# Every other partition for each of a pair's two primitives, and feed-forward biases loaded in attention

## The reference, cut to what matters

```python
def _compose_weight(logits, A, B):
    vals, idx = jax.lax.top_k(logits, 32)
    w = jax.nn.softmax(vals / 1.0)
    return jnp.einsum('k,kir,kro->io', w, A[idx], B[idx])   # A: (64, d_in, 64), B: (64, 64, d_out)

W1 = _compose_weight(fc1_logits, fc1_A, fc1_B)              # (256, 1024)
W2 = _compose_weight(fc2_logits, fc2_A, fc2_B)              # (1024, 256)
h = gelu(x @ W1)
return h @ W2
```

## Time and profile before

| | us |
|---|---|
| median of 3 runs (lowest, highest) | 1976.05 (1974.21, 1977.6) |
| the profiled execution | 1973.82 |
| its span, first to last instruction | 1972.0 |
| PE busy in the span | 1919.5 (97%) |
| DVE, ACT, POOL busy | 1345.8, 981.2, 1068.6 |
| mean granted TensorE clock | 0.988 of 2.4 GHz |

### The profile page before, as it was taken

How to read it: one execution, slowest core, us unless ns; L and a number is a source line. 1 busy time by engine, 2 the same in 40 slices (tenths; PEclk the granted TensorE clock), 3 DMA queues, 4 the chain that set the end, 5 groups by cost and what they waited for, 6 DMA issues and landing times.

```text
span 1972.0 us, 47533 instructions
## 1 busy us (share of the span) xinstructions
PE 1919.5 (97%) x19756; PEld 1579.7 (80%) x19756; DVE 1345.8 (68%) x3293; ACT 981.2 (50%) x1803; POOL 1068.6 (54%) x973
## 2 busy tenths in 40 slices
PE   8998999999999999999999879999999999999998
PEld 2335888888888888888888679999999999999997
DVE  3555566676667666776677655869686868777776
ACT  4444666776767666766676543222323222322231
POOL 1453998899889998899889201222212121312221
PEclk9997999999999999999999989999999999999999
DMA  7344200022000300021102864101010101010100
GB/s 274 123 162 164 107 34 34 34 76 76 34 34 3 117 34 34 34 76 55 34 15 69 221 160 109 44 23 43 33 35 31 44 22 44 22 44 22 44 11 22
DMA packets 26247, 128.04 MB, mean 65 GB/s; under 512 B 4592, under 2 KB 5168, under 8 KB 19888
## 3 DMA queue, kind: packets, MB, share of 16 engines
q1 hardware_dynamic: 19952, 86.53, 13.7%
q0 software_dynamic: 2304, 25.17, 3.8%
q10 hardware_dynamic: 3776, 13.30, 1.7%
HBM read 93.53 MB, written 31.46 MB: 63 GB/s over the span
## 4 chain that ended last, share of the span: by engine, by line
PE 81%; POOL 3%; DMA 2%; issue 2%; DVE 1%; ACT 1%; SPq 1%; POOLq 0%; ACTq 0%; DVEq 0%
PE bankC L32 12%; PE bankC L34 12%; PE bankC L33 12%; PE ring L32 6%; PE ring L34 6%; PE ring L33 6%; PE big L877 4%; PE big L32 3%; PE big L34 3%; PE big L33 3%; PE ring L808 3%; PE big L788 3%; PE big L884 3%; PE ring L852 2%; PE ring L830 2%
## 5 line engine op out<-in xcount | busy, mean ns | idle before, releaser
L32 PE MATMUL bankC<-down_hi,act_hi 128*128 128x256 f32 x1024 | 292.1, 285 | 0.0
L34 PE MATMUL bankC<-down_hi,act_lo 128*128 128x256 f32 x1024 | 289.5, 283 | 0.0
L33 PE MATMUL bankC<-down_lo,act_hi 128*128 128x256 f32 x1024 | 288.8, 282 | 0.0
L1490 DVE TENSOR_TENSOR act_lo<-gel,act_hi 128x512 fp32r<-128x512 f32 x256 | 210.6, 823 | 8.8
L1452 POOL TENSOR_TENSOR rstdC<-var_epsC,minus_halfC 128x4 f32<-128x4 f32 x48 | 53.9, 1122 | 281.5 <-DVE var_epsC L1515 281.5
L32 PE MATMUL bankC<-aT_hi,up_hi 128*128 128x512 f32 x512 | 204.1, 399 | 0.0
L34 PE MATMUL bankC<-aT_hi,up_lo 128*128 128x512 f32 x512 | 201.7, 394 | 0.0
L1446 POOL TENSOR_TENSOR hC<-hC,vecC 128x1024 f32<-128x1024 f32 x16 | 39.5, 2470 | 298.0 <-PE turn L1363 298.0
L33 PE MATMUL bankC<-aT_lo,up_hi 128*128 128x512 f32 x512 | 200.7, 392 | 0.0
L33 PEld LDWEIGHTS bankC<-down_lo,act_hi 128*128 128x128 f32 x1024 | 195.5, 191 | 1.4
L32 PEld LDWEIGHTS bankC<-down_hi,act_hi 128*128 128x128 f32 x1024 | 194.8, 190 | 1.4
(11 more groups left out here) (192 smaller groups left out, 5398.6 us busy)
## 6 DMA issues: line engine op xcount, KB each, us to landing
w_first<-w_split POOLq DMA_DIRECT2D x8, 1536.0 KB, 7.1
w_second<-w_split POOLq DMA_DIRECT2D x8, 1536.0 KB, 8.7
raw_late<-in_AB SPq DMA_DIRECT2D x30, 320.0 KB, 5.1
xs<-in_x_conv SPq DMA_DIRECT2D x16, 513.0 KB, 7.5
u<-hA SPq DMA_DIRECT2D x8, 1024.0 KB, 4.6
u_next<-u SPq DMA_DIRECT2D x8, 1024.0 KB, 6.0
hC<-u SPq DMA_DIRECT2D x16, 512.0 KB, 3.9
xC<-in_x SPq DMA_DIRECT2D x16, 512.0 KB, 4.8
```

Source lines behind the costliest of these rows:

```text
L32: e.matmul(out, wh, xh, start=start, stop=False)
L33: e.matmul(out, wh, xl, start=False, stop=False)
L34: return e.matmul(out, wl, xh, start=False, stop=stop)
L1490: e.tensor_tensor(a_lo[:, fb, :], g, a_hi[:, fb, :].bitcast(F32), ALU.subtract).then_inc(s_act_lo, 1)
```

## The change

Three things change.

1. Of a pair's two primitives one fills the even partitions and the other the odd ones (`to[half::2, :]`). `w_col` must follow: `vector_rest` makes a column of ones on even and one on odd partitions (`parity`) by a sum over the identity matrix, for which it waits, and forms `w_col` with six instructions in place of four. The constant `ROW` moves up by one, since one more instruction counts the semaphore up.
2. `b1s` and `vecC` get memory of their own, and their two DMAs move from ACT's list at n = 12 to SP's list, ahead of the loads of pair 0 in `prefetch`. The wait for all of attention moves to just before `first.scalar`.
3. `first.scalar(0)` and `first.vector(0)` move from n = 14 to n = 16.

```diff
--- before.py
+++ after.py
@@ -325,7 +325,8 @@
             rank.vector(e)
             for n in range(STEPS + LAG):
                 if n == LAG:
-                    rank.vector_rest(e)
+                    w.wait_ge(d_eye, 16)
+                    rank.vector_rest(e, identity)
                 if 0 <= n - LAG < STEPS:
                     keep_rows(n - LAG)
                 q, half = half_at(n)
@@ -363,6 +364,7 @@
         self.chosen, self.ones, self.euler = sb("chosen", [N, 2]), sb("onesN", [N, P]), sb("euler", [N, 2])
         self.weight, self.place = sb("weight", [N, 2, P]), sb("place", [N, 2, K])
         self.inv_sum, self.total, self.w_row = sb("inv_sum", [P, 2]), sb("total", [P, 2]), sb("w_row", [P, 2, K])
+        self.parity = sb("parity", [P, 2])
         sem = lambda n: ctx.enter_context(nc.semaphore("rank_" + n))
         self.d_in, self.s_ones, self.s_v, self.s_exp, self.s_mm = (sem(n) for n in ("in", "ones", "v", "exp", "mm"))
 
@@ -382,10 +384,10 @@
         e.wait_ge(self.s_v, self.LESS_TOP)
         e.tensor_tensor(self.expo[:, :], self.euler[:, :], self.expo[:, :], ALU.pow).then_inc(self.s_exp, 1)
 
-    LESS_TOP, PLACES, ROW = 9, 14, 15
+    LESS_TOP, PLACES, ROW = 9, 14, 16
 
     def vector(self, e):
-        v, K, R = self.s_v, self.K, P // 2
+        v, K = self.s_v, self.K
         e.wait_ge(self.d_in, 4 * 16)
         for f in range(2):
             e.tensor_scalar(self.more[:, f, :], self.row[:, f, :], self.col[:, f:f + 1], None, ALU.is_gt).then_inc(v, 1)
@@ -410,22 +412,28 @@
             e.tensor_scalar(self.place[:, f, :], self.index[:, 1:1 + K], self.rank[:, f:f + 1], None,
                             ALU.is_equal).then_inc(v, 1)
 
-    def vector_rest(self, e):
-        v, K, R = self.s_v, self.K, P // 2
+    def vector_rest(self, e, identity):
+
+        v, K = self.s_v, self.K
+        e.tensor_reduce(self.parity[:, :], identity[:, :].rearrange("p (a two) -> p two a", two=2), X, ALU.add).then_inc(v, 1)
         e.wait_ge(self.s_mm, 1)
         e.tensor_copy(self.w_row[:, :, :].rearrange("p a b -> p (a b)"), self.rows_ps[:, 0:2 * K]).then_inc(v, 1)
         e.tensor_copy(self.picks[:, :], self.picks_ps[0:1, 0:2 * K]).then_inc(v, 1)
-        e.wait_ge(v, 15)
+        e.wait_ge(v, 16)
         e.tensor_reduce(self.total[:, :], self.w_row[:, :, :], X, ALU.add).then_inc(v, 1)
-        e.wait_ge(v, 17)
+        e.wait_ge(v, 18)
         e.reciprocal(self.inv_sum[:, :], self.total[:, :]).then_inc(v, 1)
-        e.wait_ge(v, 18)
+        e.wait_ge(v, 19)
+        at = lambda f, half: self.w_row[:, f, :].rearrange("p (a two) -> p a two", two=2)[:, :, half]
         for f in range(2):
-            for half in range(2):
-                rows = slice(R * half, R * half + R)
-                e.tensor_scalar(self.w_col[rows, f, :],
-                                self.w_row[rows, f, :].rearrange("p (a two) -> p a two", two=2)[:, :, half],
-                                self.inv_sum[rows, f:f + 1], None, ALU.mult).then_inc(v, 1)
+            e.tensor_scalar(self.w_col[:, f, :], at(f, 1), self.parity[:, 1:2], None, ALU.mult).then_inc(v, 1)
+        for f in range(2):
+            e.wait_ge(v, 21 + f)
+            e.scalar_tensor_tensor(self.w_col[:, f, :], at(f, 0), self.parity[:, 0:1], self.w_col[:, f, :], ALU.mult,
+                                   ALU.add).then_inc(v, 1)
+        for f in range(2):
+            e.wait_ge(v, 23 + f)
+            e.tensor_scalar(self.w_col[:, f, :], self.w_col[:, f, :], self.inv_sum[:, f:f + 1], None, ALU.mult).then_inc(v, 1)
 
     def tensor(self, e):
         K = self.K
@@ -1169,7 +1177,7 @@
 
 
 def ffn_phase(nc, x, u_in, out, w1, b1, w2, rows2, comp, identity, w_col, picks, place, sems, before, early,
-              d_early, d_u4, x1_at, y_at):
+              d_early, d_consts, d_u4, x1_at, y_at):
     B, T, H = x.shape
     F = w1.shape[1] // (H // P)
     CB, FB = H // P, F // P
@@ -1188,13 +1196,12 @@
 
         up = [split("up0", [P, CB, F]), split("up1", [P, CB, F])]
         down = [split("down0", [P, FB, H]), split("down1", [P, FB, H])]
-        b1s = sb("b1s", [P, FB + 2 * CB])
-        vec = sb("vecC", [P, 5 * H])
+        b1s, vec = place["b1s"], place["vecC"]
         minus_half = sb("minus_halfC", [P, TILES])
         x_both, h_both = place["xC"], place["hC"]
         gel = sb("gel", [P, GEL, TOK])
         hs = [h_both[:, s, :, :] for s in range(LANES)]
-        d_consts, d_w, d_h = sem("d_consts"), [sem(f"d_w{n}") for n in range(2)], [sem(f"d_h{s}") for s in range(LANES)]
+        d_w, d_h = [sem(f"d_w{n}") for n in range(2)], [sem(f"d_h{s}") for s in range(LANES)]
         rows = lambda a: a.rearrange("p t c -> p (t c)")
         h_rows = u_in.rearrange("b p (m f) -> b m p f", m=LANES)
         pick = lambda a, b, s: a[b:b + 1, s].rearrange("a p f -> (a p) f")
@@ -1226,12 +1233,6 @@
                         w.wait_ge(s_w_lo, 1)
                         w.wait_ge(s_b1_ps, 1)
                         e.dma_start(rows(hs[s]), pick(h_rows, 0, s)).then_inc(d_h[s], 16)
-
-            @staticmethod
-            def scalar_loads(e, w):
-                wait_free(w, before.free["all"])
-                e.dma_start(b1s[:, :], b1).then_inc(d_consts, 16)
-                e.dma_start(vec[:, :], rows2.partition_broadcast(P)).then_inc(d_consts, 16)
 
             @staticmethod
             def scalar(e, n):
@@ -1589,7 +1590,7 @@
     N, R, K = src.shape[0], src.shape[1], picks.shape[1] // 2
     at = f * K + 2 * j + half
     chosen = e.value_load(picks[0:1, at:at + 1], min_val=0, max_val=N - 1)
-    e.dma_start(to[R * half:R * half + R, :], src[bass.ds(chosen, 1)].rearrange("a r n -> (a r) n")).then_inc(done, 16)
+    e.dma_start(to[half::2, :], src[bass.ds(chosen, 1)].rearrange("a r n -> (a r) n")).then_inc(done, 16)
 
 
 def compose_phase(nc, up, down, comp, w_col, picks, place, sems, before, first, early, d_early):
@@ -1623,7 +1624,7 @@
         FINISH = {2: 0, 3: 1, 4: 2, 6: 3, 7: 4, 8: 5}
         UNITS_AT = {7: 1, 11: 2}
 
-        FIRST_AT = {14: 0, 22: 1}
+        FIRST_AT = {16: 0, 22: 1}
         TAKE_AT = DUOS + 2
         BIAS_AT = DUOS + 6
         ROWS_AT = len(duos) - 3
@@ -1704,9 +1705,8 @@
                     last(0)
                 if n in UNITS_AT:
                     last(UNITS_AT[n])
-                if n == 12:
-                    first.scalar_loads(e, w)
                 if n in FIRST_AT:
+                    wait_free(w, before.free["all"])
                     first.scalar(e, FIRST_AT[n])
                 if n == TAKE_AT:
                     take(0)
@@ -1795,6 +1795,9 @@
                                  [("gkT", split_rows, F32), ("kc", [P, T // P // 2, 2 * H], F32)]])
         overlay(nc, ctx, place, [[("xC", [P, 2, T // P // 2, H], F32), ("hC", [P, 2, T // P // 2, H], F32)],
                                  [("cos_q", split_rows, F32), ("sin_q", split_rows, F32)]])
+
+        place["b1s"], place["vecC"] = sb("b1s", [P, t["b1"].shape[1]]), sb("vecC", [P, t["rows2"].shape[1]])
+        d_consts = ctx.enter_context(nc.semaphore("d_consts"))
         d_u4 = [ctx.enter_context(nc.semaphore(f"d_u4_{s}")) for s in range(2)]
 
         late = place["raw_late"]
@@ -1802,6 +1805,9 @@
         d_early = [ctx.enter_context(nc.semaphore(f"d_early{j}")) for j in range(6)]
 
         def prefetch(e, pairs):
+            if 0 in pairs:
+                e.dma_start(place["b1s"][:, :], t["b1"]).then_inc(d_consts, 16)
+                e.dma_start(place["vecC"][:, :], t["rows2"].partition_broadcast(P)).then_inc(d_consts, 16)
             for j in pairs:
                 for half in range(2):
                     load_half(e, comp, picks, 0, j, half, early[j], d_early[j])
@@ -1810,7 +1816,7 @@
                                     {n: t[n] for n in ("cos_k", "sin_k", "cos_q", "sin_q")}, t, bias_qk, bias_v, keep, place,
                                     ctx, d_u0, d_u4, prefetch)
         feed_forward = ffn_phase(nc, t["x"], t["u4"], t["out"], t["w1"], t["b1"], t["w2"], t["rows2"], comp, identity, w_col,
-                                 picks, place, ctx, attention, early, d_early, d_u4, flat(u_next), w_flat)
+                                 picks, place, ctx, attention, early, d_early, d_consts, d_u4, flat(u_next), w_flat)
 
         def sync(e):
             attention.sync(e, feed_forward.sync)
```

## The result

The changed kernel takes 1950.82 us (1948.09 to 1950.98, 4 runs), the one before 1976.82 in the same comparison: ratio 0.9867, 95% interval 0.985 to 0.9884. The forecast was 1955.5, in a range of 1951.5 to 1962. The profiled execution has a span of 1946.3 us against 1972.0.

The account below looks back on a forecast made before the run. PE, busy 97% of the span, bounds the kernel. -19.0 us for ACT's two idle stretches and -1.0 ahead of pair 31 make -20.0: 1953.8 from the profiled execution, 1956.0 from the median; forecast 1955.5, range 1951.5 to 1962.

Parts of the forecast that it names:

- The two DMAs leave ACT: Composition, pairs 12 to 16: without the DMAs on ACT, pair 16 starts at 1139.3 instead of 1158.31, 19.0 us gained.
- two stands: ACT's idle stretches in composition: 9.41 us waiting for the store, 8.98 us for two loads; both were to go.
- Ahead of pair 31: Late composition: PE's 1.01 us wait for that pair's load, in a full queue, was to go: -1.0 us.
- Pair 12 still starts at 1127.42 ... no edit touches these: Composition: ACT's pieces of the last unit wait for POOL until 1121.71, so this pair's start stays unchanged.
- The rest 0: Whole kernel: everything besides the -19.0 and -1.0 us in composition was counted as no change.
- first rival: Composition: pair loads stay at 235 GB/s, pair 15 starts 3.1 us late; -15.9 us, or 1960; chance 0.23.
- the prediction's own sign of a wrong path: Composition: wrong if a new ACT wait reaches PE, or SP's last five pairs set the end, not pair 22.
- third rival: Pair loads: every other partition is dearer; gain gone at 0.92 us more per pair, perhaps 1984 us; chance 0.08.
- The rate itself: Composition's pair loads: over 260 GB/s at share 1.0 where only they run, instead of 235.
- n = 16: Composition: the moved wait for the store costs nothing, covered by 1.3 us at path end, 1.8 for landing.
- Ranking: DVE's extra reduction and instructions: some 0.5 us, 0.8 hidden in DVE's 1.13 us wait for PE; cost nothing.

Follow-up runs that it names:

- the repetition: The changed kernel run once more with nothing altered: 1951.45 us, ratio 0.9879 to the kernel before.
- the experiment: The changed kernel with the pairs' primitives back on neighbouring partitions and w_col made as before: 1958.13 us, ratio 0.9911 to the kernel before.

## Why the prediction was off, step by step

**The two DMAs leave ACT.** Right: -19.0 forecast for pairs 12 to 16; the steps give (10.87 + 4.76 + 10.13 + 5.13) - (3 x 2.72 + 3.63) = 19.1. It took both edits: with neighbouring partitions the same steps sum to 16.4 and not 11.8. The profile of before is also the best of its kind, its four steps sum to 30.9 us where five kernels with the same two stands had 32.9 to 33.5.

**Ahead of pair 31.** The size is right, -1.0 forecast and 4.12 to 2.95 us measured, but partly by luck: in the five other kernels with the old loads and both stands PE waited 0.7, 0, 0, 0.2 and 0.2 us there, so the profile of before had the longest wait of the six.

**"Pair 12 still starts at 1127.42 ... no edit touches these".** Counted from the start of composition, wrong by 1.4 us in this profile, by 0.5 in its repetition. ACT waits there for POOL, and POOL's four small instructions, before and after, were:

```profile
1116.16 1.51 POOL L747 TENSOR_SCALAR var_epsB<-momentsB 128x4 f32<-128x4 f32 x1 [6.80 <-DVE momentsB L1101]
1117.64 1.56 POOL L748 TENSOR_SCALAR minus_mean<-momentsB 128x4 f32<-128x4 f32 x1
1119.29 1.04 POOL L751 TENSOR_TENSOR rstdB<-var_epsB,minus_halfB 128x4 f32<-128x4 f32 x1
1120.40 1.27 POOL L753 TENSOR_TENSOR offset<-minus_mean,rstdB 128x4 f32<-128x4 f32 x1
```

```profile
1116.51 1.51 POOL L755 TENSOR_SCALAR var_epsB<-momentsB 128x4 f32<-128x4 f32 x1 [7.48 <-DVE momentsB L1109]
1117.99 0.46 POOL L756 TENSOR_SCALAR minus_mean<-momentsB 128x4 f32<-128x4 f32 x1
1118.53 1.86 POOL L759 TENSOR_TENSOR rstdB<-var_epsB,minus_halfB 128x4 f32<-128x4 f32 x1
1120.47 0.20 POOL L761 TENSOR_TENSOR offset<-minus_mean,rstdB 128x4 f32<-128x4 f32 x1
```

Two of them lost over 1 us, one took 0.8 more, and the chain, begun 0.4 us later, ends 1.0 us earlier. The same instruction takes 0.20 or 1.27 us. The step from pair 11 to 12 was 2.71 to 4.17 us over all fourteen profiles, 2.72 in the kernel with the places alone and 3.67 in the repetition. So I count it as chance and not as an effect of an edit; what it depends on was not tested.

**"The rest 0".** This is the step that failed, and the larger part of the miss (the profile gained 25.7 us and not 20.0): I costed "memory of their own" by its DMAs alone. It moves `up`, `down` and attention's buffers by 5184 bytes, which is 81 times 64. Feed-forward won 5.0 us by it, shown by the kernel with the places alone. Attention lost 1.4 us from its fourth unit on, shown by the same kernel; of the +1.1 at its end the rest is the scatter of its start. The sum of what was measured, -19.1 for the stands, -1.2 ahead of pair 31, -1.4 ahead of pair 12, -5.0 in feed-forward and +1.1 up to composition, is -25.6 against -25.7.

**The price of the old DMA rate (first rival).** The rival did not come about, but its size was wrong: I gave neighbouring partitions 4.1 us, the experiment 9.6 to 10.7 in composition, about 7 in the medians. I had let the rate of 2.79 us for a pair keep up with PE from pair 15 on. In the experiment PE waits ahead of pair 16 too, and ahead of pairs 29 to 31, where SP issues the last five pairs in one row from 1170.20 to 1182 and the last loads take 8.1 us to land (4.4 in the changed kernel). That is the prediction's own sign of a wrong path, the end of composition set by SP's last five pairs. A queue that only just keeps up had no slack for such a burst.

The 17.5 us in the third rival's break-even stand nowhere else in the prediction; what its first rival leaves is 15.9, which puts the break-even at 0.84 us for a pair. Nothing hung on it.

**The rate itself.** Right: over 260 GB/s was asked for, 328 came. Alone it is worth 10 to 12 us, since both stands on ACT were DMA time; with the loads moved, 7 to 11 us. The two edits overlap: composition goes from 124.0 to 110.3 by the one, 112.8 by the other and 102.2 to 103.3 by both.

The four rows that each engine would take in sequence, which I read out of the Trainium skill ("DMA: Bandwidth & Descriptors", "Why a DMA increments its semaphore by 16 and not by 1") as a danger of engines in step, did not keep the rate at 235 to 245 GB/s; whether they are part of why it was 328 and not 403, no run shows. The port map of the Trainium skill's "SBUF — State Buffer", "Door 1: The DMA port swizzle (why [64,N] ≈ [32,N])", by which 0 to 63 reach half of the ports, agrees in direction with 245 and 328 GB/s; the factor is 1.3 and not 2, in a stretch where full-width loads run in both.

**n = 16.** Right: no new wait. `first.scalar(0)` was forecast for 1134.4 and started at 1134.07.

**Ranking.** Right: 0.44 us more of idle time used up, none reached PE.

## What to carry to other kernels

Giving a buffer a place of its own moves every buffer behind it. Compare the pitch of matmuls in stages that a change doesn't touch, and test the move alone before the rest is explained; where PE is always busy, 64 bytes between the matrix it streams and the one it loads weights from are worth a try. Loads that fill half the partitions ran faster here on every other one, and each wait on a DMA behind their queue shrank with it. Price a queue by its bursts and not by its mean.

## What the runs showed of the hardware

- Pair loads to 64 neighbouring partitions kept the queue at 235 to 245 GB/s, to every other partition at 325 to 328 (at a DMA share of 0.94 to 0.96, with a like mix of other loads), and at 407 with the store in it; landing fell from 14.3 or 14.8 us to 5.1.
- The pitch of 128x256 matmuls was 115.5 to 120.0 ns according to the places of the two operands modulo 128 bytes; that of the 128x512 matmuls of the up product was 233 ns, and 234 in the two kernels with padding between `up` and `down`. Attention answered too (775.5 to 778.1 us for 28 units), by a rule that these runs don't give.
- One and the same POOL instruction over 128x4 elements (`offset<-minus_mean,rstdB`) took 0.20 us in one profile and 1.27 in another.
- Behind the 32 matmuls of one column the granted clock fell to the lower of its two levels in thirteen of the fourteen profiles. The two steps from pair 22 to 24 took 10.4 to 10.9 us in six of them and 12.2 to 12.5 in seven, kernels among them that differ only in padding (10.5 in the kernel before, 12.4 with 2048 bytes more). In the changed kernel with neighbouring partitions the granted clock stayed at 1.00 over both steps, which took 9.3 us:

```profile
1168.80:1179.00 10.20, 10.20 (x86) 10.20 (x87) 4.20 (x6) 2.92 (x4) 0.00 (x0) 1.00 0.84 216
```
